# The output projection moved ahead of the last projections of a step, in a fused attention and expert kernel

## The reference

```python
mod = (_silu(c) @ wmod).reshape(4, 6, 1, -1)         # sa, ca, ga, sb, cb, gb
h = _layernorm(x) * (1 + ca) + sa
q, k, v = _heads(h @ wq.T), _heads(h @ wk.T), _heads(h @ wv.T)      # 16 heads of 64
phi(t) = exp(t @ omega.T - 0.5 * sum(t * t)) / sqrt(64)
kv_cumsum = cumsum(phi(k) x v);  k_cumsum = cumsum(phi(k))
out = phi(q) . kv_cumsum / (phi(q) . k_cumsum + 1e-6)
x = x + ga * (out.reshape(b, n, 1024) @ wo.T + bo)
h = _layernorm(x) * (1 + cb) + sb
x = x + gb * ffn(h)       # top 2 of 8 experts, capacity 1024 rows, 128 -> 512 -> 128 with gelu
```

## Time and profile before

| | us |
|---|---|
| median of 3 runs | 747.66 (746.46 to 751.94) |
| the profiled execution | 750.19 |
| its span, first to last instruction | 748.4 |

### The profile page before, as it was taken

One profiled execution on the slowest core, in us unless ns is written; L12 is line 12 of the kernel. 1 busy time (PEld: TensorE's weight loads), 2 busy tenths in 40 slices (PEclk: granted clock), 3 DMA queues, 4 the chain that ended last, 5 costly groups with the idle time before them and its releaser, 6 DMA issues. The chain is left out here.

```text
span 748.4 us, 27606 instructions
## 1 busy us (share of the span) xinstructions
PE 712.3 (95%) x11581; PEld 613.6 (82%) x11581; DVE 547.2 (73%) x1684; ACT 384.3 (51%) x740; POOL 337.6 (45%) x630
## 2 busy tenths in 40 slices
PE   7989999999999999999999999999998679999996
PEld 6878888888888888888888888888887669999994
DVE  6477888888888888788888788878775445655427
ACT  4555566556665556655566555655552134445310
POOL 3002444545555544444555554444446504565550
PEclk9799999999999999999999999999999999999999
DMA  9982000000000000000000000000000054454128
GB/s 259 363 314 90 9 10 11 10 10 11 9 11 13 14 10 10 11 9 10 10 11 10 10 17 9 11 10 10 10 10 10 25 169 144 135 175 137 50 83 296
DMA packets 32707, 47.27 MB, mean 63 GB/s; under 512 B 4132, under 2 KB 20168, under 8 KB 32584
## 3 DMA queue, kind: packets, MB, share of 16 engines
q1 hardware_dynamic: 23296, 32.62, 13.0%
q0 software_dynamic: 4096, 8.42, 3.5%
q10 hardware_dynamic: 5192, 4.47, 1.8%
HBM read 22.21 MB, written 23.36 MB: 61 GB/s over the span
## 5 line engine op out<-in xcount | busy, mean ns | idle before, releaser
L1265 POOL DMA_INDIRECT y_rows<-y_sb,row_id x64 | 62.8, 982 | 66.6 <-DVE y_sb L1409 50.6
L639 ACT COPY v_sb<-bank 128x512 f32<-128x512 f32 x64 | 37.6, 588 | 106.9 <-PE bank L279 103.5
L1009 POOL TENSOR_TENSOR h_lo<-h_full,h_hi 128x192 fp32r<-128x192 f32 x32 | 19.1, 597 | 141.2 <-ACT h_hi L632 141.2
L1079 POOL DMA_INDIRECT dispatched<-h_cur,slot x64 | 67.2, 1050 | 17.9 <-issue 16.1
L1343 ACT ACTIVATE hidden<-bank,b_col 128x512 f32<-128x512 f32 x64 | 43.3, 689 | 58.2 <-PE bank L1316 57.8
L623 ACT ACTIVATE phi_k<-expo_k 128x1024 f32<-128x1024 f32 x32 | 33.9, 1058 | 62.8 <-DVE expo_k L754 62.8
L515 PEld LDWEIGHTS bank<-woT,attT 128*128 128x128 f32 x512 | 61.9, 191 | 3.1 <-ACT attT L725 0.6
L515 PE MATMUL bank<-woT,attT 128*128 128x128 f32 x512 | 62.4, 275 | 0.4 <-ACT attT L725 0.4
L1285 PE MATMUL bank<-w_sb,hidden 128*128 128x128 f32 x512 | 59.7, 275 | 0.8 <-issue 0.8
L1285 PEld LDWEIGHTS bank<-w_sb,hidden 128*128 128x128 f32 x512 | 58.4, 192 | 1.2 <-issue 1.2
L754 DVE SCALAR_TENSOR_TENSOR expo_k<-norm_k,bank 128x512 f32<-128x512 f32 x64 | 44.0, 687 | 19.3 <-PE bank L279 19.2
(11 more groups left out here) (236 smaller groups left out, 2084.7 us busy)
## 6 DMA issues: line engine op xcount, KB each, us to landing
dispatched<-blank SPq DMA_DIRECT2D x16, 524.0 KB, 3.0
region<-dispatched SPq DMA_DIRECT2D x30, 262.0 KB, 2.9
y_rows<-blank SPq DMA_DIRECT2D x8, 512.0 KB, 3.5
w_nat<-in_L_ffn_w_dram SPq DMA_DIRECT2D x8, 256.0 KB, 3.5
y_got<-y_rows SPq DMA_DIRECT2D x8, 256.0 KB, 6.8
y_got<-y_rows ACTq DMA_DIRECT2D x8, 256.0 KB, 7.7
out_dram<-x_sb SPq DMA_DIRECT2D x8, 256.0 KB, 3.5
w_sb<-in_L_ffn_w_dram ACTq DMA_DIRECT2D x6, 256.0 KB, 3.2
```

Of the source, the lines that this page charges most:

```text
L1079: pool.indirect_dma_start(out=dispatched[:, :], in_=h2_cur[par][:], in_offset=None, out_offset=bass.IndirectOffsetOnAxis(ap=slot[par][:, k ...
L1265: pool.indirect_dma_start(out=y_rows[:, :], out_offset=bass.IndirectOffsetOnAxis(ap=row_id[par][:, t:t + 1].bitcast(U32), axis=0), in_=y_s ...
```

## The change

The wo product moves in PE's list: it stands directly behind `attend(0)`, then the rank, then `pk0` and `pk1`. Its result goes to bank 2 instead of bank 7, behind the transposed attended values `attT0`. So `tk0` of the next step, the next user of bank 2, waits for `wo_out` (DVE's addition of bo) where it waited for ACT's copy `attT0_out`. `state_gain(0)`, which uses banks 6 and 7, no longer waits for `wo_out`; it waits for the late and early sums and the rank to have been read. In the last step without a chunk of its own, the transposes wait for `wo_out` too. On DVE, `normalise(0)` and the addition of bo move ahead of `find_places` and of both exponents of k, which now stand together.

```diff
-                         2: ["tk0", "tk1", "a0", "attT0"], 3: ["tq0", "tq1", "a1", "attT1"],
+                         2: ["tk0", "tk1", "a0", "attT0", "wo"], 3: ["tq0", "tq1", "a1", "attT1"],
...
-                         6: ["late0", "hT", "late1", "rank"], 7: ["early0", "early1", "wo"]}
+                         6: ["late0", "hT", "late1", "rank"], 7: ["early0", "early1"]}
...
-                                    pe.wait_ge(sem(f"attT{z}_out"), c - 1)
+                                    pe.wait_ge(sem("wo_out" if z == 0 else "attT1_out"), c - 1)
...
-                                if c >= 2:
-                                    pe.wait_ge(sem("wo_out"), c - 1)
-                                elif c == 1:
-                                    pe.wait_ge(sem("gain1_out"), 1)
-                                else:
+                                if c >= 1:
+                                    pe.wait_ge(sem("gain1_out"), c)
+                                if c >= 3:
+                                    pe.wait_ge(sem("rank_out"), c - 2)
+                                if c == 0:
                                     pe.wait_ge(sem("d_chain"), 3)
...
+                            elif half == 0:
+                                pe.wait_ge(sem("wo_out"), c - 1)
...
-                            if c < NCH:
-                                pe.wait_ge(sem("gain1_out"), c + 1)
                             for t in range(NP):
...
                             attend(0, c, par, j)
-                            if front:
-                                project("pk0", c, nxt)
+                            if tail:
+                                add_heads(c)
                             if last:
                                 routing_rank(c)
                             if front:
+                                project("pk0", c, nxt)
                                 project("pk1", c, nxt)
-                            if tail:
-                                add_heads(c)
...
                                 state_add(1)
-                            if front:
-                                exponent("k", 0, c)
-                            if last and c != NCH:
-                                find_places()
-                            if front:
-                                exponent("k", 1, c)
-                            if back:
                                 normalise(0, c)
                             if tail:
                                 dve.wait_ge(sem("x2_ready"), times(c - 1))
                                 dve.wait_ge(sem("wo_in"), c)
                                 dve.tensor_tensor(upd[0][:], psum[BANK["wo"]][:, 0:D], bo_b[:], ALU.add).then_inc(sem("wo_out"), 1)
+                            if last and c != NCH:
+                                find_places()
+                            if front:
+                                exponent("k", 0, c)
+                                exponent("k", 1, c)
```

## The result

The changed kernel takes **771.49 us** (median of 4 runs, 769.88 to 772.25) against 747.56 us (median of 4) for the kernel before: 1.030 times as long, with a 95% interval of 1.026 to 1.034. It is slower by 23.9 us where 12.9 were forecast. The range that the prediction gives the forecast itself, 756 to 765, is missed by 6.5 us. Its wide range ends at 771, and the time lies 0.5 us above that; as a ratio to the kernel before, 1.030 lies just under the 1.031 of 771 to 747.66. In the later comparisons, with 7 to 20 runs of the kernel before, its median was 748.7 to 749.5 us, so some 1 to 2 of the 23.9 us are probably the luck of four runs.

What follows compares the result with a forecast made beforehand. PE looks saturated, but ACT's `phiT_k` decides when each step's first scores start. 30 x 0.41 = 12.3 plus 0.6 is 12.9 us, on 747.66 gives 760.5 us; own range 756 to 765, wide range 753 to 771.

Steps and rivals of the forecast that it cites:

- Step 1: PE from attend(0) to the last product of `pk1`: with the wo product and rank ahead, `pk1` ends 1.58 us later.
- Step 2: DVE ahead of the `k` exponents: normalise and the addition moved there stay hidden by PE's products, by 0.2 us.
- Step 3: From the last product of `pk1` to the first scores: 6.32 us without the wo product, read from kernel step 0.
- Step 4: Sum per kernel step: scores 0.41 us later; `phi_k` 1.58 later, ACT gets back 1.17, its queue is the bound.
- Step 5: Possible gains from the update's addition coming about 1.7 us earlier, and from the rank's wait going: worth nothing.
- Step 6: One-time cost in kernel step 0, where normalise now stands ahead of DVE's exponents: 0.6 us.
- The rival that had more of the delay staying: ACT's run wins back only its 0.61 us pause: 0.97 us a step, 29 us, 777; chance 0.13.
- The rival without a difference: PE stays the bound with the same products, ACT's delay is hidden: 747.7 us, within 7 either way; chance 0.08.

## Why the prediction was right or wrong

The direction and the place of the loss were right, and so was the chain over `phi_k`; that a second chain of the same length stood beside it was missed, and the size was half.

*Step 1, when PE reaches the end of pk1*: forecast 1.58 us later, measured 3.75 - 1.99 = 1.76. The term that was sized wrong is the wo product, 1.70 us. Behind `pk1` it ran from 404.22 to 405.92, but its first weights had been loaded under the last product of `pk1`, and what follows it, a projection, shows its start early and then takes 0.32 us to its second product instead of 0.23. Behind attend(0) the first load stands free, and from the product's start to the rank's it is 419.90 - 418.01 = 1.89. A start-to-start distance belongs to its two neighbours; it doesn't move unchanged with the instruction. The prediction added the 1.70 unchanged; that was its largest mis-sized term, 0.18 us in each step, 5 us in all. `attT` was no part of it.

*Step 2, DVE*: right. The exponent waits for PE, 0.41 us, so it was hidden with more room than the 0.2 worked out, and `phi_k` follows `pk1` by 1.30 as before. The run with DVE's old order shows that the new one even helps, by 0.2 us a step.

*Step 3, pk1 to the scores*: forecast 6.32 from step 0, measured 1.30 + 5.01 = 6.31. One unusual step of the kernel before showed what every step of the change would do, to 0.01 us.

*Step 4*: the size of what is won back was right (1.19 for 1.17), the reason was not complete. It says that the change leaves ACT's queue as the bound. The runs with half of `phi_k` and with `tq0` first show that ACT's run and PE's road behind the wait of `q0` end together: shorten either and the other holds (2.5 us less, 1.4 us more), shorten both and 10.0 us come back. The 0.44 us for which `q0` waits stood in the prediction, inside the 6.32 of step 0, but was not taken for a bound; it is the other half of the loss's explanation, not another loss. For the stretch behind the scores, where the order does stay the same, the sum had nothing; there 0.09 us a step were added, 2.6 us, and that stays unexplained.

*Step 5, gains*: none showed, as said. *Step 6*: attend(0) to `phi_k` in step 0 took 3.60 instead of 3.17 us, 0.43 for the 0.6 forecast.

The sum by the measured terms: 30 x (1.76 - 1.19 + 0.09) = 19.8, and 0.4 for step 0 makes 20.2, against 19.7 between the spans. The rival that had more of the delay staying (0.97 us a step, 29 us) comes nearer in time (23.9) than the forecast, but not by its mechanism: ACT did win back what step 0 said. The rival without a difference, by which PE's unchanged work decides, is refuted. The Trainium skill, "Perfetto Trace Analysis", section "Identifying the Most-Contended Engine", has the busiest engine as the place to work on; here its work stayed the same product for product (11,581), and an order that exposes two hand-overs between engines cost 3%.

That the wide range came within 0.5 us is partly luck: its high end was set for the slower rival, whose mechanism did not happen, and not for the terms that were too small. Its low end, called half of the addition, would be 754.1 and not 753. Of the 11.0 us between forecast and median, 4.2 are no error in the terms: the profiled execution of before was 2.6 us slower than its median, that of the change 1.6 faster. By the spans the time would have been 747.66 + 19.7 = 767.4. The other 6.8 us are mainly the wo product (5 us) and the stretch behind the scores (2.6 us), less a few tenths by which points 4 and 6 came out better than forecast.

## What to carry to other kernels

Work that seems free to move on a busy engine may be what hides the next two engines' chain: before it is moved, follow the chain that starts behind it (here `pk1`, exponent, exponential, squares, copies, scores) and look for a step in the same trace in which it is missing; that step is the new kernel. When a wait in front of one instruction is found, shorten two suspects together as well as each alone; two roads of one length look like no cause in single tests. And read the difference of the usual steps apart from the mean, since rare pauses can be worth as much as the edit.

## What the runs showed that was not expected

Some steps are 0.4 to 2.4 us longer than the usual one, by pauses of PE in front of which no engine is late. They come at a few places of the program: between the `phi_k` of steps 16 and 17, 19 and 20, 26 and 27, 29 and 30, with the wo product ahead also behind those of steps 4, 9 and 14, and in some kernels behind those of steps 1 and 11 (1.1 us behind step 1 in the change). Each of the eleven kernels whose page counts 27606 or 27635 instructions has three to seven such steps, with lengths that vary (behind step 26: 2.0 us in the kernel before, 1.1 with half of its `phi_k`, none with the shared bank alone). The three kernels with 27574 instructions have one of 0.4 us between them, and each gained 3.6 to 4.9 us although their usual steps stayed equal to 0.02 us. So taking out the four waits together took nearly all of the pauses away, three times. A smaller count alone does not: the change with one wait less has 27606 instructions, 29 fewer than the change, and seven such steps. The differences in the counts are all in PE's waiting instructions (505, 537 and 566 of them). Why the pauses are there, the trace doesn't say, and whether it is the number of instructions, where they come to lie, or which waits are gone was not told apart.

A product of the projections (512 columns, one record each in the trace) follows the one before it by 0.23 us, but the first one behind another kind of product has 0.32 us to the next. Nine ACT instructions in a row, with nothing to wait for, took 4.96 us from the start of `phi_k` to the end of the last `phiT_k` (422.48 to 427.44), though their durations add up to more: each starts about 0.1 us before the one ahead of it ends.
